# Attention on one Trainium2 core: sums of the softmax taken from the product with the values, copied and gathered off TensorE, with the transfers of one queue in another order

## The chip, the cores and the metric

The kernel runs on one core of a Trainium2 chip, as a single launch. The metric is device time in microseconds (us), and less is better. The engines named below are TensorE (PE; its weight loads are shown apart as PEld), VectorE (DVE), ScalarE (ACT), GpSimd (POOL) and SyncE (SP), whose queue here issues nearly all transfers of the stage that is changed.

## What is computed

The program is a small model of two layers: causal attention, a gated feed-forward net with 2:4 sparsity, a state space layer, and a mixture of experts, each behind a layer norm and added to its input. Only the first attention is touched: 8 sequences of 512 tokens, width 256, 16 heads of 16 columns.

```python
q = jnp.concatenate([q_sem, q_geo], axis=-1)
k = jnp.concatenate([k_sem, k_geo], axis=-1)
scores = jnp.einsum('bhqd,bhkd->bhqk', q, k).astype(jnp.float32) * scale
scores = jnp.where(causal, scores, jnp.finfo(jnp.float32).min)
attn = jax.nn.softmax(scores, axis=-1).astype(v.dtype)
out = jnp.einsum('bhqk,bhkd->bhqd', attn, v)
out = out.transpose(0, 2, 1, 3).reshape(B, S, ATTN_DIM)
return out @ Wo.T
```

## The kernel before

**Tiling.** `causal_attention` takes a batch (512 tokens) in two halves, f = 0 and 1, of 8 heads each. A half has four steps, t = 0 to 3, one for each pair of heads. Steps 0 and 1 belong to the first quad of four heads, steps 2 and 3 to the second. A step has three fills, j = 0 to 2, which share out the tiles of a 512 by 512 lower triangle. The middle six batches are a hardware loop over b with eight steps in it; the first and the last batch and two halves ahead of them are written out.

**What a step does.** PE writes the scores of this pair turned (keys on the partitions) into `p_st` (`turned_scores`, L384 in the trace), DVE limits the diagonal (`keep_past`, L580), and ACT takes the exponential into `pt_a`, `pt_b` or `pt_c` (`exponential`, L522). `p_st` is one buffer, so the turned scores of fill j + 1 wait for the exponential of fill j. Between them PE computes the scores of the pair two steps later the other way round (`scores`, L374 and L377, into `p_s`), and DVE takes their row maxima (`maximum`, L573).

**The path of the maxima.** A maximum has to stand in two extra rows of `qs` when its pair's turned scores begin. GpSimd splits it in two parts, DVE turns these (`turn_maxima`, L587, into `trn`), and SP moves them out to `max_dram` (`maxima_out`, L267) and back into rows of `qs` (`maxima_in`, L277). The first turned scores of a step wait for that.

**Queries and keys** of the next half go the same way: three transfers of a split projection to DRAM (`spread_rows`, L255), then two back (`stack`, L262) into `qs` or `ks`. All of them stand in SP's queue in the order of the code, and a wait in it holds up all that is behind. In step 0 SP issues the maxima out, the stack of the queries, the maxima in and the spread of the keys; in step 1 the maxima out, the stack of the keys, the maxima in.

**Values and sums.** `weigh` (L414) multiplies the exponentials of a quad by its values into `p_o`, and by `ones` into `p_sum`. It runs for fill 0 at the end of steps 1 and 3, and for fills 1 and 2 in the step behind. In step 0 of the next half DVE takes the reciprocal of `p_sum` in two parts (L625, L633) and multiplies `p_o` by it into `ot` (L636). The output product of a batch (`project_out`, L422) follows in steps 2 and 3 of the half f = 0 of the next batch, into the banks a and c, and `add_residual` (L600) adds the input. In step 3 it waits for ACT's copies of the turned values out of bank c (`v_pad`, L543).

In the profile the program's names have the prefix `a_`: `a_psst` is `p_st`, `a_pss` `p_s`, `a_pso` `p_o`, `a_pssum` `p_sum`, `a_psa` and `a_psb` the banks a and c.

## Time and profile before

| what | us |
| --- | --- |
| median of three runs | 6276.34 (6274.32 to 6280.89) |
| the profiled execution, whole | 6271.52 |
| its span | 6269.7 |
| first scores of the attention to its last output product | 95.78 to 803.06 |
| PE busy in the stretch 155 to 765 | 533.57 of 610.00 |
| DVE, ACT, POOL busy in it | 368.07, 178.62, 89.51 |

The attention is about a ninth of the span. The rest of the program has the same code in both kernels. In a view by time (the timeline) a row gives the start, the length, the engine and line, and in brackets how long the engine had been idle and which engine or transfer ended that. The rows of SPq are issues of transfers: their length is that of the issue, not of the transfer.

### The profile page before, as it was taken

How to read it: one execution, taken by the hardware profiler on the slowest of the kernel's cores; microseconds unless marked ns; L12 is line 12 of the kernel's file. 1: busy time of each engine (PE TensorE's matmuls, PEld its weight loads, DVE VectorE, ACT ScalarE, POOL GpSimd, SP SyncE). 2: the span in 40 equal slices, each digit the busy share in tenths (PEclk: the TensorE clock that was granted, in tenths of full speed). 3: DMA queues.
4: the chain of work that ended last, by engine and by line, in shares of the span. 5: the costliest groups of instructions: out<-in, count | busy, mean ns of one | idle time of the engine just before them, and what ended most of it. 6: DMA issues, size and time to landing. Idle time of an engine off the chain costs nothing. (4 is left out here: it accounts for less than half of the span.)

```text
span 6269.7 us, 129594 instructions
## 1 busy us (share of the span) xinstructions
PE 5619.0 (90%) x41820; PEld 4006.3 (64%) x41820; DVE 4504.9 (72%) x6855; ACT 3469.1 (55%) x4692; POOL 3610.0 (58%) x4085
## 2 busy tenths in 40 slices
PE   5888858747999999999999999999999999985599
PEld 3444447535777777777777777777777777763487
DVE  4666555545888888888888888888888888844444
ACT  2233222134777777777777777777777777731122
POOL 2111100005888888888888888888888888830000
PEclk8899779868999999999999999999999999987799
DMA  3333210122111111111111111111111111122100
GB/s 91 91 93 84 68 61 24 47 71 66 31 28 33 29 30 28 32 29 30 29 30 32 28 31 28 32 29 30 28 33 29 30 28 31 29 77 74 42 24 20
DMA packets 428605, 263.10 MB, mean 42 GB/s; under 512 B 264740, under 2 KB 359524, under 8 KB 427652
## 3 DMA queue, kind: packets, MB, share of 16 engines
q1 hardware_dynamic: 420100, 253.98, 15.7%
q10 hardware_dynamic: 8448, 8.39, 0.4%
q8 instruction: 32, 0.52, 0.0%
q14 instruction: 25, 0.20, 0.0%
HBM read 186.73 MB, written 66.85 MB: 40 GB/s over the span
## 5 line engine op out<-in xcount | busy, mean ns | idle before, releaser
L1537 ACT ACTIVATE ss_r<-ss_pssum,ss_eps 128x512 f32<-128x512 f32 x512 | 352.8, 689 | 900.5 <-PE ss_pssum L1468 900.5
L1597 DVE SCALAR_TENSOR_TENSOR ss_psb<-ss_psb,ss_norm,ss_r 128x512 f32<-128x512 f32 x512 | 362.8, 754 | 446.2 <-ACT ss_r L1539 446.2
L1468 PE MATMUL ss_pssum<-ss_sq,ss_pairssum 128*128 128x512 f32 x1024 | 570.9, 639 | 57.1 <-DVE ss_fr L1585 57.0
L1349 POOL TENSOR_TENSOR ss_sq<-ss_sq 128x512 f32<-128x512 f32 x256 | 329.7, 1288 | 452.5 <-ACT ss_sq L1546 452.5
L48 PE MATMUL ss_psb<-x_hi,ss_whi 128*128 x1024 | 529.5, 517 | 4.4 <-DVE ss_fr L1585 4.4
L1449 PE MATMUL ss_psse<-ss_rot 64*128 64x128 f32 x8224 | 529.4, 279 | 1.2 <-POOL ss_rot L1331 1.2
L1379 POOL TENSOR_TENSOR ss_own<-ident,ss_tk 128x512 f32<-128x512 f32 x512 | 524.8, 1047 | 0.0
L1449 PEld LDWEIGHTS ss_psse<-ss_rot 64*128 64x128 f32 x8224 | 480.1, 188 | 44.4 <-issue 42.9
L48 PE MATMUL ss_psc<-x_hi,ss_whi 128*128 x1024 | 504.9, 493 | 0.0
L50 PE MATMUL ss_psb<-x_hi,ss_wlo 128*128 x1024 | 404.1, 395 | 0.0
L49 PE MATMUL ss_psc<-x_lo,ss_whi 128*128 x1024 | 403.6, 394 | 0.0
L1339 POOL TENSOR_TENSOR ss_sq<-ss_sq 128x512 f32<-128x512 f32 x256 | 325.1, 1270 | 135.0 <-ACT ss_sq L1553 135.0
L50 PE MATMUL ss_psc<-x_hi,ss_wlo 128*128 x1024 | 402.2, 393 | 0.0
L49 PE MATMUL ss_psb<-x_lo,ss_whi 128*128 x1024 | 402.0, 393 | 0.0
L1304 POOL MEMSET ss_rot<- 128x4096 f32 x1 | 3.5, 3512 | 669.5 <-POOLq L2018 669.5
L1458 PE MATMUL ss_psm<-ss_xe,ss_bt 128*128 128x16 f32 x3084 | 388.9, 264 | 0.0
L1458 PEld LDWEIGHTS ss_psm<-ss_xe,ss_bt 128*128 128x128 f32 x3084 | 363.9, 191 | 31.2 <-issue 0.2
L1597 DVE SCALAR_TENSOR_TENSOR ss_psc<-ss_psc,ss_norm,ss_r 128x512 f32<-128x512 f32 x512 | 361.5, 752 | 0.0
L1619 DVE TENSOR_TENSOR ss_gm<-ss_psse,ss_dec 128x1024 f32<-128x1024 f32 x257 | 314.7, 1224 | 41.7 <-POOL ss_dec L1340 41.7
L1539 ACT ACTIVATE ss_r<-ss_r 128x512 f32<-128x512 f32 x512 | 324.1, 633 | 16.3
L1373 POOL TENSOR_TENSOR ss_rot<-ss_rot,ss_tmp 128x512 f32<-128x512 f32 x256 | 333.0, 1301 | 0.0
L1519 ACT ACT_TABLE_LOAD x257 | 329.7, 1283 | 4.5
(354 smaller groups left out, 15646.1 us busy)
## 6 DMA issues: line engine op xcount, KB each, us to landing
ss_dtb<-time_steps SPq DMA_DIRECT2D x516, 128.0 KB, 2.8
ss_wraw<-in_w_state SPq DMA_DIRECT2D x264, 80.0 KB, 2.3
head_rows<-a_yhi SPq DMA_DIRECT2D x64, 256.0 KB, 3.5
a_qs<-head_rows SPq DMA_DIRECT2D x32, 384.0 KB, 5.7
a_ks<-head_rows SPq DMA_DIRECT2D x32, 384.0 KB, 5.6
ss_xp<-x_heads SPq DMA_DIRECT2D x33, 256.0 KB, 4.2
y_heads<-ss_yo SPq DMA_DIRECT2D x132, 64.0 KB, 2.4
head_rows<-a_ylo SPq DMA_DIRECT2D x32, 256.0 KB, 3.7
```

What stands on the lines that cost most here:

```text
L48: nc.tensor.matmul(out, w_hi, x_hi, start=first, stop=False)
L49: nc.tensor.matmul(out, w_hi, x_lo, start=False, stop=False)
L50: return nc.tensor.matmul(out, w_lo, x_hi, start=False, stop=last)
L1349: G.tensor_tensor(sq[:, 0, 0], sq[:, 0, 0], sq[:, 0, 1], ALU.add).then_inc(ss_b, 1)
L1373: G.tensor_tensor(rot[:, j, 0], rot[:, j, 0], tmp[:, 0, 0], ALU.add)
L1379: last = G.tensor_tensor(own[:, h * TPB:(h + 1) * TPB], g.ident[:].rearrange("p (o t) -> p o t", o=1).broadcast_to([P, TPB, P]), at_diagon ...
L1449: last = M(p_se[:, h * TPB + c, :], rot[at, 1 - j, e, cols], rot[at, 1 - j, 2 + e, cols], start=e == 0, stop=e == 1)
L1458: last = M(p_m[:, (c * 2 + e) * PW:(c * 2 + e + 1) * PW], bt[:, 2 if e else j, c, :], xe[:, 1 - j, c, :], start=True, stop=True)
L1468: M(p_sum[:], pairs_sum[:], sq[:, q, 0], start=True, stop=True).then_inc((sum_b, sum_c)[q], 1)
L1519: A(trig[:, j, 0], fr[:], ACT.Sin, scale=UNDER_TURN)
L1537: A(r[:, q], p_sum[:], ACT.Ln, scale=1.0 / N1, bias=eps[:, 0:1]).then_inc(ln, 1)
L1597: link.mark(S(bank[:, e, :], bank[:, e, :], norm[:, 2 * q + e:2 * q + e + 1], r[:, q], ALU.mult, ALU.mult))
```

## The change

**Values and sums in one product.** `v_pad` is filled with 1.0, so the 16 columns beside a head's values give its sum. Each quad has a bank of its own (`p_o[0]`, `p_o[1]`), and the product with `ones` is gone. What is left has values and sums in alternate strips of 16 rows.

**Normalisation.** ACT copies a quad's bank to `o_sb`, and once more, times a column of zeros and ones, to `o_own` (`take`), in step 3 for the first quad and in step 0 of the next half for the second. SP moves the sums to their values' rows by four transfers a quad (`gather_sums`). GpSimd adds the two parts of `o_own` (step 1), DVE takes the reciprocals, one at the end of step 1 and one in step 2, and multiplies in step 2.

**Maxima.** DVE turns them right behind the first `keep_past` of a step, ahead of the first `maximum`. They come in by two transfers of two rows instead of four of one, and ahead of the stack of the queries. The stack of the keys moves from step 1 to step 0, behind the spread of the keys.

**Output.** `project_out` now runs in step 3 of f = 0 and step 0 of f = 1, both into bank c; the store moves from step 0 to step 1 of f = 1. One more step is written out at the end.

```diff
@@ -203,3 +203,6 @@
         vt, v_pad = sb("vt", [P, SEQ]), sb("vpad", [P, TPB, 2, 2, 4, 2 * DH])
-        ones, nil = sb("ones", [P, 2, 2 * DH]), sb("nil", [P, 2, TPB])
+        nil = sb("nil", [P, 2, TPB])
+        o_sb, sums = sb("osb", [P, 2, SEQ]), sb("sums", [P, SEQ])
+        o_own, o_all = sb("oown", [P, 2, SEQ]), sb("oall", [P, SEQ])
+        strips, own = sb("strips", [P, 2, 4]), sb("own", [P, 2])
         rec, ot = sb("rec", [P, SEQ]), sb("ot", [P, KD, SEQ])
@@ -208,3 +211,3 @@
         p_st, p_s = ps("st", [P, 2, SEQ]), ps("s", [P, 2, SEQ])
-        p_o, p_sum = ps("o", [P, SEQ]), ps("sum", [P, SEQ])
+        p_o = [ps(f"o{q}", [P, SEQ]) for q in range(2)]
         p_ab = [ps(n, [P, SEQ]) for n in "ab"]
@@ -235,2 +238,3 @@
                 step(BATCH, 0, t, BATCH)
+            step(BATCH, 1, 0, BATCH)
 
@@ -274,6 +278,11 @@
                 for e in range(2):
-                    for s in range(2):
-                        at = 64 * e + KS + s
-                        sp.dma_start(qs[at:at + 1, f, u, :].bitcast(FP32).rearrange("o (i a r) -> o i a r", i=TPB, a=TPB),
-                                     columns[8 * e + 4 * s:8 * e + 4 * s + 4].unsqueeze(0)).then_inc(max_in[p], 16)
+                    at = 64 * e + KS
+                    sp.dma_start(qs[at:at + 2, f, u, :].bitcast(FP32).rearrange("s (i a r) -> s i a r", i=TPB, a=TPB),
+                                 columns[8 * e:8 * e + 8].rearrange("(s i) a r -> s i a r", s=2)).then_inc(max_in[p], 16)
+
+            def gather_sums(half, quad):
+                sp.wait_ge(o_copied, half * 2 + quad + 1)
+                for c in range(4):
+                    to, at = 32 * c + DH * quad, 32 * c + DH * (1 - quad)
+                    sp.dma_start(sums[to:to + DH, :], o_sb[at:at + DH, quad, :]).then_inc(sums_in, 16)
 
@@ -284,4 +293,2 @@
                     maxima_out(b, 4 * f + t + 1)
-                if t < 2 and is_half(half + 1):
-                    stack(*after, t)
                 if is_pair(4 * half + t + 1):
@@ -289,6 +296,12 @@
                 if t == 0 and is_half(half + 1):
+                    stack(*after, 0)
                     spread_rows(*after, 1)
+                    stack(*after, 1)
                 if t == 2 and is_half(half + 2):
                     spread_rows(b + 1, f, 0)
-                if f == 1 and t == 0 and 1 <= n < BATCH:
+                if t == 3 and is_half(half):
+                    gather_sums(b * 2 + f, 0)
+                if t == 0 and is_half(half - 1):
+                    gather_sums(b * 2 + f - 1, 1)
+                if f == 1 and t == 1 and 1 <= n < BATCH:
                     before = b - 1
...
@@ -313,3 +326,3 @@
             G.memset(top2[:].bitcast(FP32), 0.0)
-            G.memset(v_pad[:], 0.0).then_inc(cleared, 1)
+            G.memset(v_pad[:], 1.0).then_inc(cleared, 1)
             G.memset(qs[:].bitcast(FP32), 0.0).then_inc(cleared, 1)
@@ -335,2 +348,6 @@
                     rest(*after, 1)
+                if t == 1 and is_half(half - 1):
+                    pool.wait_ge(o_masked, (b * 2 + f) * 2)
+                    at_least(pool, ot_done, b * 2 + f - 1)
+                    G.tensor_tensor(o_all[:], o_own[:, 0], o_own[:, 1], ALU.add).then_inc(merged, 1)
                 if t == 1 and is_half(half + 2):
...
@@ -411,6 +428,5 @@
                     width = SEQ - kt * P
-                    for psum, left in ((p_o, lambda c: v_pad[:, kt, f, quad, c, :]), (p_sum, lambda c: ones[:, quad, :])):
-                        for c in range(4):
-                            last = M(psum[32 * c:32 * c + 32, kt * P:SEQ], left(c), pt[:, c // 2, c % 2, at:at + width],
-                                     start=quad == 0 and j == 0, stop=quad == 1 and j == 2, skip_group_check=True)
+                    for c in range(4):
+                        last = M(p_o[quad][32 * c:32 * c + 32, kt * P:SEQ], v_pad[:, kt, f, quad, c, :], pt[:, c // 2, c % 2, at:at + width],
+                                 start=j == 0, stop=j == 2, skip_group_check=True)
                 last.then_inc(pv_done, 1)
...
@@ -444,3 +460,3 @@
                     project(b + 1, f * HALF, a).then_inc(proj_done, 1)
-                if t == 3 and outs:
+                if f == 0 and t == 3 and outs:
                     if is_half(half + 1):
@@ -448,6 +464,4 @@
                     pe.wait_ge(ot_done, b * 2)
-                    project_out(b, 1, c)
+                    project_out(b, 0, c)
                 if t == 3 and is_half(half + 2):
-                    if outs:
-                        pe.wait_ge(res_done, b * 2 - 1)
                     pe.wait_ge(rope_read, counts(2) + 1)
@@ -462,16 +476,15 @@
                     weigh(ef, eq, 2)
+                if f == 1 and t == 0 and outs:
+                    if is_half(half + 1):
+                        pe.wait_ge(rope_read, counts(1) + 4)
+                    pe.wait_ge(res_done, b * 2 - 1)
+                    project_out(b, 1, c)
                 if t == 1 and is_half(half + 2):
                     at_least(pe, rope_read, counts(1) + 4)
+                    if f == 1 and outs:
+                        pe.wait_ge(res_done, b * 2)
                     project(b + 1, f * HALF + P, c).then_inc(proj_done, 1)
-                if t == 2 and outs:
-                    if is_half(half + 2):
-                        pe.wait_ge(rope_read, counts(2) + 1)
-                    if is_half(half + 1):
-                        pe.wait_ge(vt_ready, b * 2 + f + 2)
-                    at_least(pe, res_done, b * 2 - 2)
-                    pe.wait_ge(ot_done, b * 2)
-                    project_out(b, 0, a)
                 if t == 3 and is_half(half + 2):
-                    if outs:
-                        pe.wait_ge(res_done, b * 2)
+                    if f == 0 and outs:
+                        pe.wait_ge(res_done, b * 2 - 1)
                     at_least(pe, vpad_done, b * 2 + f + 2)
@@ -488,3 +501,3 @@
                         pe.wait_ge(vpad_done, b * 2 + f + 1)
-                        at_least(pe, ot_done, b * 2 + f)
+                    at_least(pe, o_masked, b * 4 + f * 2 - 1 + t // 2)
                     weigh(f, t // 2, 0)
...
@@ -523,2 +537,9 @@
 
+            def take(half, quad):
+                act.wait_ge(pv_done, (half * 2 + quad + 1) * FILLS)
+                at_least(act, rec_done, half)
+                at_least(act, merged, half)
+                A(o_sb[:, quad], p_o[quad][:], ACT.Copy).then_inc(o_copied, 1)
+                A(o_own[:, quad], p_o[quad][:], ACT.Copy, scale=own[:, quad:quad + 1]).then_inc(o_masked, 1)
+
             def high(b, f, kind):
@@ -534,2 +555,4 @@
                     exponential(b, f, t, 0)
+                if t == 3 and here:
+                    take(b * 2 + f, 0)
                 if t == 0 and is_half(half + 1):
@@ -548,2 +571,4 @@
                     exponential(b, f, t, 2)
+                if t == 0 and is_half(half - 1):
+                    take(b * 2 + f - 1, 1)
                 if t == 0 and is_half(half + 1):
@@ -561,6 +586,8 @@
             V.tensor_scalar(limit[:], above_f[:, 1, :], 1.5e38, 2.0, ALU.add, ALU.mult).then_inc(t_loaded, 1)
-            V.memset(ones[:], 0.0).then_inc(t_loaded, 1)
-            dve.wait_ge(t_loaded, 51)
-            V.memset(ones[:, 0, 0:DH], 1.0)
-            V.memset(ones[:, 1, DH:2 * DH], 1.0).then_inc(t_loaded, 1)
+            for q in range(2):
+                V.tensor_reduce(strips[:, q], g.ident[:].rearrange("p (c w) -> p c w", w=2 * DH)[:, :, DH * q:DH * (q + 1)], AX.X, ALU.add).then_inc(t_loaded, 1)
+            dve.wait_ge(t_loaded, 52)
+            for q in range(2):
+                last = V.tensor_reduce(own[:, q:q + 1], strips[:, q], AX.X, ALU.add)
+            last.then_inc(t_loaded, 1)
 
...
@@ -604,3 +631,3 @@
                 ahead = is_pair(4 * half + t + 2)
-                outs = f == 0 and 1 <= n <= BATCH
+                outs = 1 <= n <= BATCH
                 here = is_half(half)
@@ -608,8 +635,8 @@
                     keep_past(b, f, t, 0)
-                if ahead:
-                    maximum(b, f, t, 0)
                 if is_pair(4 * half + t + 1):
                     turn_maxima(b, 4 * f + t + 1)
-                if t == 3 and outs:
-                    add_residual(b, 1)
+                if ahead:
+                    maximum(b, f, t, 0)
+                if f == 0 and t == 3 and outs:
+                    add_residual(b, 0)
                 if here:
@@ -622,16 +649,19 @@
                     turn(b + 1, f, t // 2, 1)
-                if t == 0 and is_half(half - 1):
-                    dve.wait_ge(pv_done, (b * 2 + f) * 2 * FILLS)
-                    V.reciprocal(rec[:, 0:SEQ // 2], p_sum[:, 0:SEQ // 2])
+                if f == 1 and t == 0 and outs:
+                    add_residual(b, 1)
+                if t == 2 and is_half(half - 1):
+                    V.reciprocal(rec[:, SEQ // 2:SEQ], sums[:, SEQ // 2:SEQ]).then_inc(rec_done, 1)
                 if here:
                     keep_past(b, f, t, 2)
-                if t == 2 and outs:
-                    add_residual(b, 0)
                 if ahead:
                     maximum(b, f, t, 2)
-                if t == 0 and is_half(half - 1):
-                    V.reciprocal(rec[:, SEQ // 2:SEQ], p_sum[:, SEQ // 2:SEQ]).then_inc(rec_done, 1)
+                if t == 1 and is_half(half - 1):
+                    dve.wait_ge(sums_in, (b * 2 + f) * 128)
+                    at_least(dve, ot_done, b * 2 + f - 1)
+                    V.reciprocal(rec[:, 0:SEQ // 2], sums[:, 0:SEQ // 2])
+                if t == 2 and is_half(half - 1):
                     at_least(dve, wo_done, b * 2 if f else b * 2 - 2)
+                    dve.wait_ge(merged, b * 2 + f)
                     dve.wait_ge(rec_done, b * 2 + f)
-                    V.tensor_tensor(ot[:, 1 - f, :], p_o[:], rec[:], ALU.mult).then_inc(ot_done, 1)
+                    V.tensor_tensor(ot[:, 1 - f, :], o_all[:], rec[:], ALU.mult).then_inc(ot_done, 1)
 
```

SP's queue in the hardware loop, from the end of the maxima in of step 0 to those of step 1 in the first half. `maxima` and `head_rows` are scratch tensors in DRAM; a wait for `ln0_stats` is one for the split projection (a number used again). Before:

```order
L277 DMA a_qs<-maxima 1x16x32 x3
L252 REGISTER_ALU
L255 DMA head_rows<-a_yhi 128x512 [waits ln0_stats]
L255 DMA head_rows<-a_yhi 128x512
L255 DMA head_rows<-a_ylo 128x512
L266 REGISTER_ALU
L267 DMA maxima<-a_trn 128x32 [waits a0_turned]
L262 DMA a_ks<-head_rows 48x4x512 [waits a0_kspread]
L262 DMA a_ks<-head_rows 48x4x512
L272 ISA
L277 DMA a_qs<-maxima 1x16x32 [waits a0_maxout0]
L277 DMA a_qs<-maxima 1x16x32 x3
```

After, from the spread of the keys on; the maxima in of step 0 and the stack of the queries stand right ahead of it:

```order
L259 DMA head_rows<-a_yhi 128x512 [waits ln0_stats]
L259 DMA head_rows<-a_yhi 128x512
L259 DMA head_rows<-a_ylo 128x512
L266 DMA a_ks<-head_rows 48x4x512 [waits a0_kspread]
L266 DMA a_ks<-head_rows 48x4x512
L284 ISA
L287 DMA a_sums<-a_osb 16x512 [waits a0_ocopied]
L287 DMA a_sums<-a_osb 16x512 x3
L270 REGISTER_ALU
L271 DMA maxima<-a_trn 128x32 [waits a0_turned]
L276 ISA
L280 DMA a_qs<-maxima 2x16x32 [waits a0_maxout0]
```

The stack of the keys, with its wait for the spread, and the gathering of the sums moved ahead of the maxima out of step 1.

DVE in the same loop, the change from step 0 to step 1, before (waits for `a0_st` are for turned scores, those for `ln0_hi` for scores):

```order
L633 RECIPROCAL a_rec<-a_pssum 128x256
L218 REGISTER_ALU
L636 TENSOR_TENSOR a_ot<-a_pso,a_rec 128x512 [waits a0_rec,a0_wo]
L577 ISA
L580 TENSOR_TENSOR a_psst<-a_psst,a_limit 128x2x128 [waits a0_st]
L569 ISA
L573 TENSOR_REDUCE a_top<-a_pss 128x2 [waits a0_mlo,ln0_hi]
L573 TENSOR_REDUCE a_top<-a_pss 128x2
L218 ISA [waits a0_mlo]
L587 STREAM_TRANSPOSE a_trn<-a_top 128x32 [waits a0_maxout0]
```

After, the change from step 1 to step 2:

```order
L607 TENSOR_TENSOR a_psst<-a_psst,a_limit 128x2x128 [waits a0_st]
L596 REGISTER_ALU
L600 TENSOR_REDUCE a_top<-a_pss 128x2 [waits ln0_hi]
L659 ISA
L221 REGISTER_ALU [waits a0_sumsin]
L661 RECIPROCAL a_rec<-a_sums 128x256 [waits a0_ot]
L607 TENSOR_TENSOR a_psst<-a_psst,a_limit 128x2x128 [waits a0_st]
L612 REGISTER_ALU
L614 STREAM_TRANSPOSE a_trn<-a_top 128x32 [waits a0_maxout1,a0_mlo]
L596 ISA
L600 TENSOR_REDUCE a_top<-a_pss 128x2 [waits a0_mlo,ln0_hi]
L600 TENSOR_REDUCE a_top<-a_pss 128x2
```

The transpose moved from behind the step's two first reductions to ahead of them, and a reciprocal with a wait for the gathered sums now stands at the end of step 1.

## Rows read from the trace of the kernel before

**Rows 1.** Windows: span, busy time of PE, PEld, DVE, ACT, POOL; clock, DMA.

```profile
155.00:765.00 610.00, 533.57 (x3756) 279.72 (x3748) 368.07 (x623) 178.62 (x238) 89.51 (x167) 0.88 0.36 86
...
460.40:474.70 14.30, 14.29 (x52) 6.79 (x52) 6.05 (x11) 2.65 (x3) 1.68 (x3) 0.53 0.33 62
```

**Rows 2.** Waits of PE from 155 to 765: total us, times, longest.

```profile
PE a_psst L384 <- DMA a_qs<-maxima: 55.4, 28, 3.4
PE a_psb L422 <- ACT a_vpad L543: 7.4, 7, 1.1
```

**Rows 3.** Timeline of PE: first turned scores of a step, each row one step.

```profile
217.18 0.50 PE L384 MATMUL a_psst<-a_qs,a_ks 50*128 50x512 f32 x2 [0.59 <-DMA a_qs<-maxima]
...
388.45 0.50 PE L384 MATMUL a_psst<-a_qs,a_ks 50*128 50x512 f32 x2
...
397.53 0.49 PE L384 MATMUL a_psst<-a_qs,a_ks 50*128 50x512 f32 x2 [0.21 <-ACT a_ptc L522]
...
410.38 0.49 PE L384 MATMUL a_psst<-a_qs,a_ks 50*128 50x512 f32 x2
...
421.61 0.49 PE L384 MATMUL a_psst<-a_qs,a_ks 50*128 50x512 f32 x2 [2.87 <-DMA a_qs<-maxima]
...
432.51 0.50 PE L384 MATMUL a_psst<-a_qs,a_ks 50*128 50x512 f32 x2 [0.97 <-DMA a_qs<-maxima]
...
440.80 0.50 PE L384 MATMUL a_psst<-a_qs,a_ks 50*128 50x512 f32 x2 [0.92 <-DMA a_qs<-maxima]
...
449.36 0.50 PE L384 MATMUL a_psst<-a_qs,a_ks 50*128 50x512 f32 x2
...
460.41 0.50 PE L384 MATMUL a_psst<-a_qs,a_ks 50*128 50x512 f32 x2 [2.68 <-DMA a_qs<-maxima]
...
474.74 0.53 PE L384 MATMUL a_psst<-a_qs,a_ks 50*128 50x512 f32 x2
...
728.79 0.49 PE L384 MATMUL a_psst<-a_qs,a_ks 50*128 50x512 f32 x2 [1.55 <-DMA a_qs<-maxima]
```

**Rows 4.** Timeline of PE: products with ones, and a third fill's turned scores.

```profile
416.23 0.39 PE L384 MATMUL a_psst<-a_qs,a_ks 50*128 50x256 f32 x2 [0.35 <-ACT a_ptb L522]
...
430.50 1.04 PE L414 MATMUL a_pssum<-a_pta,a_ones 128*32 128x512 f32 x8
...
472.87 1.93 PE L414 MATMUL a_pssum<-a_pta,a_ones 128*32 128x512 f32 x8
```

**Rows 5.** Timeline of SP's queue: issues of transfers in three steps and ahead.

```profile
80.39 0.81 SPq L262 DMA_DIRECT2D a_qs<-head_rows  x2
...
88.70 0.81 SPq L262 DMA_DIRECT2D a_ks<-head_rows  x2
...
413.42 0.32 SPq L267 DMA_DIRECT2D maxima<-a_trn  x1
413.87 0.83 SPq L262 DMA_DIRECT2D a_qs<-head_rows  x2
...
425.01 0.91 SPq L262 DMA_DIRECT2D a_ks<-head_rows  x2
426.06 2.57 SPq L277 DMA_DIRECT2D a_qs<-maxima  x4
435.56 0.35 SPq L267 DMA_DIRECT2D maxima<-a_trn  x1
437.01 2.57 SPq L277 DMA_DIRECT2D a_qs<-maxima  x4
```

**Rows 6.** Timeline of PE: start of the first scores of the stage.

```profile
95.48 0.37 PE L374 MATMUL a_pss<-a_above,ident 128*128 128x128 bf16 x2 [12.96 <-DMA a_ks<-head_rows]
```

**Rows 7.** Timelines of DVE and ACT: a limit, a reciprocal and a copy.

```profile
410.92 0.43 DVE L580 TENSOR_TENSOR a_psst<-a_psst,a_limit 128x256 f32<-128x256 f32 x1 [1.45 <-PE a_psst L384]
...
416.08 1.75 DVE L625 RECIPROCAL a_rec<-a_pssum 128x256 f32<-128x256 f32 x1
418.77 0.60 ACT L552 ACTIVATE a_vt<-a_psa 128x512 f32<-128x512 f32 x1
```

More of the change, by code:

```diff
@@ L178, in causal_attention @@
     s_done, max_done, mhi_done, mlo_done = sem("s"), sem("max"), sem("mhi"), sem("mlo")
-    keep_done = sem("keep")
+    keep_done, o_copied, sums_in, o_masked, merged = (sem(n) for n in ("keep", "ocopied", "sumsin", "omasked", "merged"))
     st_done, exp_done, pv_done, rec_done, ot_done = sem("st"), sem("exp"), sem("pv"), sem("rec"), sem("ot")
@@ L305, in _ @@
             for p in range(2):
-                sp.wait_ge(max_in[p], PAIRS0 // 2 * 64)
+                sp.wait_ge(max_in[p], PAIRS0 // 2 * 32)
         @block.gpsimd
@@ L400, in turned_scores @@
                 if j == 0:
-                    pe.wait_ge(max_in[t % 2], b * 256 + ((4 * f + t) // 2 + 1) * 64)
+                    pe.wait_ge(max_in[t % 2], b * 128 + ((4 * f + t) // 2 + 1) * 32)
                 at_least(pe, exp_done, (b * 8 + 4 * f + t) * FILLS + j)
@@ L501, in _ @@
             pe.wait_ge(w_split, 4)
-            pe.wait_ge(t_loaded, 16 * 3 + 4)
+            pe.wait_ge(t_loaded, 16 * 3 + 5)
             pe.wait_ge(cleared, 3)
@@ L515, in _ @@
             act.wait_ge(cleared, 3)
+            act.wait_ge(t_loaded, 16 * 3 + 5)
             def exponential(b, f, t, j):
@@ L599, in add_residual @@
                 rows = out[:, part * 2:part * 2 + 2, :]
-                V.tensor_tensor(rows, p_ab[part][:].rearrange("p (n d) -> p n d", n=2), rows, ALU.add).then_inc(res_done, 1)
+                V.tensor_tensor(rows, p_ab[1][:].rearrange("p (n d) -> p n d", n=2), rows, ALU.add).then_inc(res_done, 1)
             def step(b, f, t, n):
@@ L604, in step @@
                 ahead = is_pair(4 * half + t + 2)
-                outs = f == 0 and 1 <= n <= BATCH
+                outs = 1 <= n <= BATCH
                 here = is_half(half)
@@ L608, in step @@
                     keep_past(b, f, t, 0)
+                if is_pair(4 * half + t + 1):
+                    turn_maxima(b, 4 * f + t + 1)
                 if ahead:
                     maximum(b, f, t, 0)
-                if is_pair(4 * half + t + 1):
-                    turn_maxima(b, 4 * f + t + 1)
-                if t == 3 and outs:
-                    add_residual(b, 1)
+                if f == 0 and t == 3 and outs:
+                    add_residual(b, 0)
                 if here:
```

## The prediction

> **What bounds the kernel now.** The view by windows comes first: over most of the attention PE is busy 533.57 of 610.00 us, at a mean clock of 0.88, DVE 368.07, the others less [rows 1]. So PE is the first bound, and what it waits for is the second: 28 waits for the maxima's rows of `qs`, 55.4 us in all, and 7 for the copies of `v_pad`, 7.4 us [rows 2]. The timeline puts them in place [rows 3]. A batch takes 85.3 us (six periods from 217.18 to 728.79); I work in the one from 388.45 to 474.74, 86.29 us. Steps 2 and 3 of f = 0 take 9.08 and 12.85. Then steps 0 and 1 of f = 1 take 22.13 together, with waits of 2.87 and 0.97 for the maxima at their ends; steps 2 and 3 take 8.29 (0.92 of it such a wait) and 8.56; steps 0 and 1 of the next batch take 25.38.
>
> Why are the maxima late at the end of step 0? In SP's queue their way in stands behind the stack of the queries [rows 5]: out at 413.42, the stack at 413.87, and the step waits until 421.61. In step 1 it is behind the stack of the keys (425.01): the maxima are issued from 426.06 to 428.63, and step 2 starts at 432.51, 3.9 us later. With no stack ahead (437.01) it was 440.80, 1.2 us after the last issue ended. So transfers of one queue land about in order.
>
> A wait is followed by a low clock. Step 1 from 460.41, behind a wait of 2.68, ran at a mean clock of 0.53, mostly the lower of the levels 1.2 and 2.4 GHz [rows 1], and took 14.33 where the one from 421.61 took 10.90, of which 0.97 was a wait.
>
> **Products with ones (gain).** A product with ones of 512 columns costs PE some 0.9 us (1.04 with its tail) at full clock and 1.9 at the lower [rows 4]. A quad has three such lots: fill 0, fill 1 (384 + 128 columns) and fill 2 (256 columns, half the price). For fill 0 and fill 1 PE is the last to be ready, so 0.9 each comes off; for fill 2 the next turned scores wait 0.35 for an exponential already [rows 4], and nothing comes off.
>
> **Steps 2 and 3.** The maxima are turned earlier and come in by two issues, which takes away the wait of 0.92: 8.29 - 0.92 - 0.87 = 6.5. Against that a reciprocal of 1.75 [rows 7] now stands ahead of the third `keep_past`, where DVE has about 0.5 free: +1.25. Step 2 becomes 7.8. In f = 0 it is the same, since the output product left that step: 9.08 to 7.8. Step 3 of f = 1: 8.56 - 0.9 + 0.1 (the exponential is next in line) = 7.75. In step 3 of f = 0 the output product waits for `v_pad` [rows 2], and ACT now makes two copies of 0.6 [rows 7] ahead of it: 12.85 - 0.9 + 1.2 = 13.15.
>
> **Steps 0 and 1.** Were PE the bound, step 0 of f = 1 would take 11.23 - 2.87 - 0.9 + 1.1 (the output product moved here, less the lot and the wait that it covers) = 8.6, step 1 10.90 - 0.97 - 0.95 = 9.0, together 17.6; 16.4 in f = 0. But SP's queue has to be walked through. Count from the start of step 0. The limit starts 0.54 later and takes 0.43 [rows 3, 7]; with the transpose, the maxima go out at 1.2 (3.04 before). In 1.45 later [rows 5], at 2.65; two issues of 0.64 end at 3.95. Step 1 has its maxima in time: that wait goes. Stack of the queries at 4.0. Then come the spread of the keys and the stack of the keys, which waits for the spread. At the head of the stage the same sequence stands bare: queries at 80.39, keys at 88.70, 8.3 us later [rows 5]. So the stack of the keys is issued at 12.3. It landed 6.8 later there (95.48) [rows 6], here at 19.1. Behind it are four issues of `gather_sums`, at the stack's 0.46 each, and only then, at 15.0, the maxima out, which land behind the stack: about 19.5. In from 19.5; with two issues, landing 1.9 behind the start of the last: 22.1. **Step 2 starts 22.2 us after step 0**, in both halves, whatever PE saved. What comes off PE in these two steps, and the first wait, come back as one wait of 4.6 to 5.8 us at the end of step 1. DVE's reciprocal there waits for the sums (landed by about 20) and is done by 22, under the same wait; on GpSimd the merge is ahead of `total`, in time by 10 us. Bounds: with 1.28 for an issue of two rows, twice that of one, 24.1; if the maxima were not held behind the stack, 15.0 + 1.45 + 0.64 + 1.9 = 19.0. I take 0.64, by the nearest row.
>
> The Trainium skill, page "DMA: Bandwidth & Descriptors", section "Why a DMA increments its semaphore by 16 and not by 1", says that a transfer runs on the largest number of engines up to 16 that divides the slowest dimension of both sides. By it two rows would use 2 engines where one row of 4 by 4 pieces used 4, which speaks against joining the rows: I estimate 0.5 us later on each way in, 6283 in all; no trace here shows it.
>
> **The clock (loss).** The new wait is longer than those of 2.7 to 2.9 that the low clock followed, and what follows it is step 2. The lower level makes PE's work some 1.44 times as long (14.33 to 9.93). In step 2 it is the bound for the first third and has slack behind: +2.0 if the whole step is slow, 0 if none, +4.5 if step 3 is slow too. I take 2.0, since step 1 was slow throughout after one such wait and in part after another.
>
> **Sum.** One batch: 7.8 + 13.15 + 22.2 + 7.8 + 7.75 + 22.2 = 80.9, against 86.29, and the period is 1.0 longer than the mean: 4.4 less. The clock gives back 4.0. So 0.4 less a batch, 3 us in 7.5 batches. At the end, `take`, gathering and two output products in one bank cost some 2 us more. That makes 6271.5 - 1 = 6270.5 for the profiled execution; the median is 4.8 above it: **6275 us, no change**.
>
> **Rivals.**
> 1. The likeliest: the wait moves to the end of step 1, with a clock cost of 1.2 to 2.8 a half. 6263 to 6287. Chance 0.40.
> 2. Slower, by the clock: behind the long wait steps 2 and 3 both run at the lower level, 4.5 a half instead of 2.0: 2.5 x 15 = 37 us more, 6312. For it: the 14.33 of the step from 460.41. Against: the step from 421.61 recovered. It decides from about 8 us of low clock after the wait. Chance 0.15.
> 3. Slower, by the issue: two rows cost 1.28 in an issue: 24.1 instead of 22.2, 1.9 x 15 = 28 us, 6303. For it: an issue has the same number of small pieces a row. Chance 0.16.
> 4. Faster, by the clock: it stays up, or falls within the wait and is back: 0.4 a half, 1.6 x 15 = 24 us less, 6251. Chance 0.15.
> 5. Faster, by the transfers: the maxima aren't held up by the stack of the keys. Steps 0 and 1 take 19.0, 48 us less, and a gap of 2 us costs the clock half: 6275 - 48 - 15 = 6212. Against it: the 3.9 us of 428.63 to 432.51. Chance 0.14.
>
> **How the numbers follow.** A measurement of this kernel can tell 0.2%, 12.6 us, from no change. Faster by more than that: cases 4 and 5 and a little of 1, 0.30. Slower: 2 and 3 and a little of 1, 0.33. Within: 0.37. The range 6235 to 6316 leaves out case 5 and the far part of 2; case 1 alone has 6263 to 6287.
>
> **What would show it.** Right: no wait for maxima at the start of step 1, one of 4 to 6 us at the start of step 2; 22 us from step 0 to step 2; the stack of the keys issued some 12 us into step 0; the maxima out of step 1 issued only after the gathering. Steps 2 near 8 and 10 by the clock. Wrong: step 2 starting 18 to 20 us after step 0 (case 5), issues of the maxima well over 0.64 (case 3), a clock of 1.0 in step 2 (case 4), a wait of DVE for the gathered sums that turned scores then wait for, or a `v_pad` wait much over 2.3.

## The result, and the profile after

The changed kernel took 6326.14 us (median of four runs, 6324.81 to 6330.77) against 6275.33 for the kernel before in the same job: a ratio of 1.0083, with a 95% interval of 1.0068 to 1.0098. It is slower by 51 us, where no change was forecast, and 10 us beyond the end of the range. Its profiled execution has a span of 6323.0.

The first view is again that by windows: span, busy time of PE, PEld, DVE, ACT and POOL, then the clock, the share of the transfer engines and GB/s. The first row is most of the attention, the second steps 0 and 1 of one half, the third steps 2 and 3 behind them.

```profile
155.00:800.00 645.00, 512.37 (x2822) 267.51 (x2823) 362.59 (x615) 208.27 (x294) 112.22 (x180) 0.74 0.37 86
431.40:454.40 23.00, 16.19 (x106) 9.00 (x106) 12.95 (x22) 7.36 (x10) 5.14 (x10) 0.91 0.57 114
454.40:474.90 20.50, 19.77 (x98) 9.78 (x98) 12.83 (x22) 7.42 (x11) 3.03 (x4) 0.60 0.30 94
```

PE has less work, 79% of the time against 87%, and the mean clock of the stage fell from 0.88 [rows 1] to 0.74. Steps 2 and 3 ran at 0.60. The waits of PE from 155 to 800 (total, times, longest):

```profile
PE a_psst L401 <- DMA a_qs<-maxima: 102.8, 14, 9.2
PE a_psb L438 <- ACT a_vpad L566: 10.6, 7, 1.5
```

And one of DVE, in the same view:

```profile
DVE a_rec L661 <- DMA a_sums<-a_osb: 64.9, 14, 6.5
```

This second one lies under the first: DVE's reciprocal of the gathered sums, in its timeline, is over at 497.09, and step 2 starts at 498.30, when the maxima have landed.

```profile
495.34 1.75 DVE L661 RECIPROCAL a_rec<-a_sums 128x256 f32<-128x256 f32 x1 [3.97 <-DMA a_sums<-a_osb]
```

The 28 waits for the maxima, 55.4 us in a window 35 us shorter [rows 2], have become 14, one for each half in the window, with nearly twice the time. The timeline of PE gives their place: the first turned scores of the steps of one batch, to be laid beside [rows 3].

```profile
406.16 0.79 PE L401 MATMUL a_psst<-a_qs,a_ks 50*128 50x512 f32 x2 [6.33 <-DMA a_qs<-maxima]
...
416.38 0.80 PE L401 MATMUL a_psst<-a_qs,a_ks 50*128 50x512 f32 x2 [0.69 <-ACT a_ptc L536]
...
431.34 0.51 PE L401 MATMUL a_psst<-a_qs,a_ks 50*128 50x512 f32 x2
...
439.87 0.50 PE L401 MATMUL a_psst<-a_qs,a_ks 50*128 50x512 f32 x2
...
454.44 0.80 PE L401 MATMUL a_psst<-a_qs,a_ks 50*128 50x512 f32 x2 [6.82 <-DMA a_qs<-maxima]
...
464.66 0.80 PE L401 MATMUL a_psst<-a_qs,a_ks 50*128 50x512 f32 x2 [0.69 <-ACT a_ptc L536]
...
474.87 0.50 PE L401 MATMUL a_psst<-a_qs,a_ks 50*128 50x512 f32 x2
...
483.24 0.79 PE L401 MATMUL a_psst<-a_qs,a_ks 50*128 50x512 f32 x2
...
498.30 0.80 PE L401 MATMUL a_psst<-a_qs,a_ks 50*128 50x512 f32 x2 [6.79 <-DMA a_qs<-maxima]
```

Step 1 (439.87, 483.24) begins without a wait. Step 2 (406.16, 454.44, 498.30) begins 23.1 to 23.4 us after step 0, behind a wait of 6.3 to 6.8 (6.3 to 9.2 over all 14), at the lower clock: 0.79 to 0.80 for an instruction that takes 0.50 at the upper one. SP's queue from the same step 0 (474.87) on shows what the maxima waited for:

```profile
476.00 0.32 SPq L271 DMA_DIRECT2D maxima<-a_trn  x1
477.41 1.35 SPq L280 DMA_DIRECT2D a_qs<-maxima  x2
478.90 0.82 SPq L266 DMA_DIRECT2D a_qs<-head_rows  x2
479.84 0.84 SPq L259 DMA_DIRECT2D head_rows<-a_yhi  x2
480.72 0.48 SPq L259 DMA_DIRECT2D head_rows<-a_ylo  x1
487.50 0.81 SPq L266 DMA_DIRECT2D a_ks<-head_rows  x2
488.45 2.45 SPq L287 DMA_DIRECT2D a_sums<-a_osb  x4
491.01 0.51 SPq L271 DMA_DIRECT2D maxima<-a_trn  x1
495.45 1.33 SPq L280 DMA_DIRECT2D a_qs<-maxima  x2
```

The queue stands from 481.2 to 487.50 for the spread of the keys. The maxima out, turned by 484.62, go at 491.01, behind the stack of the keys and the gathering, and take 4.4 us to land instead of the 1.45 of [rows 5].

| one batch, us | forecast | measured |
| --- | --- | --- |
| steps 0 and 1, f = 1 and f = 0 | 22.2 and 22.2 | 23.2 and 23.5 |
| steps 2, both | 15.6 and the clock | 20.4 |
| step 3, f = 1 and f = 0 | 7.75 and 13.15, and the clock | 10.1 and 14.6 |
| of this, beyond the 36.5 that steps 2 and 3 have without the clock by the forecast | 4.0 | 8.6 |
| sum | 84.9 | 91.7 |

The measured numbers are means over the six or seven halves of a kind between 198 and 772; the sum before was 85.3.

### The profile page after: what moved, and what is told of

The parts are those of the page before. It is cut to its first block and busy times, and to the rows that moved or that the text cites. A ratio compares the mean times of both kernels' runs of the same rounds, so it can differ in the third digit from the quotient of the medians.

```text
span 6323.0 us, 127791 instructions
## 1 busy us (share of the span) xinstructions
PE 5605.9 (89%) x40796; PEld 3999.4 (63%) x40796; DVE 4505.2 (71%) x6856; ACT 3501.7 (55%) x4756; POOL 3631.5 (57%) x4101
## 3 DMA queue, kind: packets, MB, share of 16 engines
q1 hardware_dynamic: 423428, 258.18, 16.3%
## 5 line engine op out<-in xcount | busy, mean ns | idle before, releaser
L1569 ACT ACTIVATE ss_r<-ss_r 128x512 f32<-128x512 f32 x512 | 324.0, 633 | 16.4
```

## The experiments

**Which theories.** The first: step 2 waits since the maxima stand behind the stack of the keys in SP's queue. The second: what makes steps 2 and 3 longer than forecast is the clock, and PE's idle time and lighter work set it. Rivals: the added copies, gathered sums and reciprocals hold the steps; PE's total work decides the time. Unused products, where an experiment has them, are further matrix products that PE writes into a free bank and nobody reads. The experiments ran in three groups, each beside the kernel before, whose medians there were 6277.08, 6276.81 and 6281.66 us; so a difference of a few us between runs of different groups says nothing.

**Order in the queue alone, in the kernel before.**

```diff
-                if t < 2 and is_half(half + 1):
-                    stack(*after, t)
...
                 if t == 0 and is_half(half + 1):
+                    stack(*after, 0)
                     spread_rows(*after, 1)
+                    stack(*after, 1)
```

> The kernel before with the changed order in SP's queue alone: maxima in ahead of the stack of the queries, the stack of the keys in step 0 behind the spread of the keys; products with ones, reciprocals, turn of the maxima and the four issues a maximum as before. Theory 1: step 2 starts about 26 us after step 0 (maxima out at 3.0, in to 7.0, keys at 15.4, landed 22.2, maxima in 22.7, landed 26.5) instead of 22 to 24, and steps 2 and 3 run at the lower clock: a batch some 11 to 15 us longer, the whole 6355 to 6390 us. Rival (the order in the queue costs nothing, the rest of the change is what costs): within 10 us of the kernel before.

It took 6358.9 us, a ratio to the kernel before of 1.0137 (1.0110 to 1.0163). PE's first turned scores of steps 0 and 2, in its timeline:

```profile
401.97 0.49 PE L384 MATMUL a_psst<-a_qs,a_ks 50*128 50x512 f32 x2
...
428.67 0.79 PE L384 MATMUL a_psst<-a_qs,a_ks 50*128 50x512 f32 x2 [8.90 <-DMA a_qs<-maxima]
...
451.37 0.50 PE L384 MATMUL a_psst<-a_qs,a_ks 50*128 50x512 f32 x2
...
478.87 0.80 PE L384 MATMUL a_psst<-a_qs,a_ks 50*128 50x512 f32 x2 [9.69 <-DMA a_qs<-maxima]
```

26.7 and 27.5 us from step 0 to step 2, with 26 expected. The total is in the expected range, but steps 2 and 3 do not both run at the lower clock. PE's waits for the maxima from 155 to 765, then three windows: 200 to 700, step 2 and step 3.

```profile
PE a_psst L384 <- DMA a_qs<-maxima: 113.6, 14, 11.2
```
```profile
200.00:700.00 500.00, 383.64 (x2768) 198.23 (x2757) 265.44 (x454) 131.38 (x176) 69.19 (x126) 0.87 0.32 77
428.67:439.97 11.30, 11.09 (x84) 5.72 (x85) 5.01 (x10) 3.17 (x4) 1.27 (x1) 0.77 0.20 72
439.97:451.37 11.40, 10.29 (x62) 5.91 (x62) 6.88 (x13) 3.20 (x5) 2.05 (x5) 1.00 0.01 2
```

The waits are longer than in the changed kernel, and yet the mean clock is 0.87. In 11 of 13 halves the clock is back 4.7 to 6.4 us into step 2 and stays up in step 3; in the changed kernel it stays low for 15 to 20 us from the start of step 2. This kernel still has the products with ones. None of the new copies or sums is in this kernel. The order of one queue alone costs 82 us; the rest of the change, with that order given, wins 33 of them back.

**The stack of the keys back in step 1, in the changed kernel.**

```diff
                     spread_rows(*after, 1)
+                if t == 1 and is_half(half + 1):
                     stack(*after, 1)
```

> The changed kernel with one move in SP's queue: the stack of the keys goes back to step 1, behind that step's maxima in; all else stays. Theory 1 (the maxima of step 1 are held behind the stack of the keys and the gathering): the wait of 6 to 9 us ahead of step 2 goes, at most 1 to 2 us are left there (keys themselves, landing 6.8 us after their issue), the clock stays near 0.95 in steps 2 and 3, a batch takes 72 to 76 us instead of 91.5, the whole about 6190 to 6210 us. Rival (the copies, the gathered sums or the reciprocals hold the steps): a wait of DVE for the sums or one of PE for ACT takes the place, a batch stays above 82 us, the whole above 6260 us.

6302.92 us, 1.0041 (1.0028 to 1.0053): 23 us better than the changed kernel, 100 short of what was expected. PE's waits:

```profile
PE a_pss L392 <- DMA a_ks<-head_rows: 66.1, 14, 5.4
PE a_psst L402 <- ACT a_ptc L537: 9.5, 14, 0.7
PE a_psst L402 <- DMA a_qs<-maxima: 9.5, 7, 2.5
```

The maxima are in time, or late by 0.8 to 2.5 us in half of the halves, as theory 1 has it. But now the keys are not: they are issued 6 us into step 1 (437.06, step 1 at 431.00), and the scores of step 2 wait until 443.64. That was named as 1 to 2 us and measured as 2.6 to 5.4. And the clock did not come back: 0.75 from 200 to 700. The rival's totals (a batch above 82 us, the whole above 6260) came true, but not its cause, that new work holds the steps: DVE's wait for the gathered sums is down to 0.7 us in all.

**The maxima first in both steps, in the kernel before.**

```diff
                 if is_pair(4 * half + t + 1):
                     maxima_out(b, 4 * f + t + 1)
-                if t < 2 and is_half(half + 1):
-                    stack(*after, t)
                 if is_pair(4 * half + t + 1):
                     maxima_in(b, 4 * f + t + 1)
+                if t < 2 and is_half(half + 1):
+                    stack(*after, t)
```

> The kernel before with the maxima in ahead of the stack in both steps, 0 and 1; the stack of the keys stays in step 1; nothing else. The waits for the maxima of 2.9 and 1.0 us go; the keys are issued 4 us after the maxima out of step 1 instead of 0.4 and land about 11 us later, where step 2's scores want them after 10.9: a wait of 1 to 3 us for the keys at step 2 takes the place. Steps 0 and 1 together 20 to 22 us instead of 22 to 25.4, the clock about as before since PE's work is the same: 6235 to 6265 us. Rival (the clock falls with the wait for the keys): the same as before or slower.

6344.87 us, 1.0107 (1.0090 to 1.0124), a miss by 80 us. SP's queue, step 1 having begun at 402.31:

```profile
406.26 0.32 SPq L267 DMA_DIRECT2D maxima<-a_trn  x1
410.44 2.57 SPq L277 DMA_DIRECT2D a_qs<-maxima  x4
413.05 0.93 SPq L262 DMA_DIRECT2D a_ks<-head_rows  x2
```

With the wait of step 0 gone, the maxima out of step 1 (406.26) meet the stack of the queries and the spread of the keys, which are still moving: 4.2 us to land, where I counted 1.4. The keys are issued 10.7 us into step 1 instead of the 4 expected, and PE waits for them and for the maxima:

```profile
PE a_pss L374 <- DMA a_ks<-head_rows: 68.6, 13, 5.7
PE a_psst L384 <- DMA a_qs<-maxima: 37.7, 15, 4.3
```

106 us against 55.4 [rows 2]. So the stack ahead of the maxima was no oversight of the kernel before: three bulk transfers and two small ones have to pass one after another, and this order, with the small ones first, pushes the bulk back by a round trip to DRAM.

**The clock: unused products ahead of step 2, in the changed kernel.** In this edit and in the others with unused products, the product is the same, with another number and, ahead of step 1, bank `c` and a wait for `counts(1) + 4`.

```diff
+                if t == 2 and here and is_half(half + 2):
+                    pe.wait_ge(rope_read, counts(2) + 1)
+                    for _ in range(28):
+                        M(a[:], w_hi[:, 0, 0:P], g.x_hi[:, 0, 0:SEQ], start=True, stop=True)
                 if here:
                     turned_scores(b, f, t, 0)
```

> The changed kernel with 28 products of 512 columns more, about 6 us at full clock, which PE computes into a free bank ahead of step 2 in 14 of 16 halves, while it would wait for the maxima; nothing uses them. SP's order stays. Theory of the clock (steps 2 and 3 lose some 4 us a half to the lower clock behind the wait): from step 0 to step 2 still 23 us, but steps 2 of 7.8 to 8.5 instead of 10.2 us, steps 3 of 7.8 instead of 10.1 in f = 1 and about 13 in f = 0, clock near 1.0 there, the whole some 45 to 60 us shorter than the changed kernel: 6265 to 6280 us. Rival (steps 2 and 3 are long because of the added work on ACT and DVE, not of the clock): steps stay at 10, the whole the same as the changed kernel or slower.

6284.32 us, 1.0009 (0.9999 to 1.0019): 42 us less than the changed kernel, with more work on PE and the same queue. In PE's timeline, the unused products, then steps 2 and 3:

```profile
424.76 6.64 PE L454 MATMUL a_psa<-x_hi,a_whi 128*128 128x512 f32 x28
431.93 0.49 PE L401 MATMUL a_psst<-a_qs,a_ks 50*128 50x512 f32 x2 [0.53 <-DMA a_qs<-maxima]
...
439.70 0.80 PE L401 MATMUL a_psst<-a_qs,a_ks 50*128 50x512 f32 x2 [1.27 <-ACT a_ptc L540]
```

The window from 200 to 700, by the columns of the first view:

```profile
200.00:700.00 500.00, 455.11 (x2668) 267.36 (x2666) 300.31 (x510) 169.38 (x240) 95.86 (x150) 0.91 0.41 95
```

Step 2 takes 7.7 to 7.8 us in 11 of 14 halves (8.7 and 8.8 in two), just what the forecast had without the clock, where the changed kernel takes 10.2. Step 3 falls short of what was expected: 9.2 to 11.9 us in f = 1 and 13.5 to 14.2 in f = 0, instead of 7.8 and 13. In each of these the clock falls again, though no wait for the maxima is longer than 2.1 us. Only in the first half of all does it stay up through step 3, which takes 7.8 us. The two windows are that step 3 and a later one, both without an output product:

```profile
143.01:150.81 7.80, 7.70 (x45) 4.16 (x46) 5.87 (x12) 4.26 (x7) 1.44 (x3) 1.00 0.14 35
439.70:451.58 11.88, 11.88 (x46) 6.43 (x46) 6.33 (x12) 4.26 (x7) 1.70 (x3) 0.57 0.17 51
```

So the clock is worth at least 42 us here, most of it in steps 2.

**The products with ones alone, out of the kernel before.** This run leaves the sums of the softmax out; the reciprocals read the bank of the values.

```diff
-                    for psum, left in ((p_o, lambda c: v_pad[:, kt, f, quad, c, :]), (p_sum, lambda c: ones[:, quad, :])):
+                    for psum, left in ((p_o, lambda c: v_pad[:, kt, f, quad, c, :]),):
...
-                    V.reciprocal(rec[:, 0:SEQ // 2], p_sum[:, 0:SEQ // 2])
+                    V.reciprocal(rec[:, 0:SEQ // 2], p_o[:, 0:SEQ // 2])
```

> The kernel before without the products with ones (the sums are left out: the reciprocals read the bank of the values instead), the order of the queue unchanged. Theory 1 (PE's relief is lost where the maxima are awaited): PE's work falls by 70 us, but steps 0 and 1 stay at 22 to 24 us; only the steps without such a wait shrink, by 0.9 each: 15 to 35 us less, 6240 to 6260 us. Rival (PE is the bound throughout): 50 to 70 us less, 6205 to 6225 us.

6296.22 us, 1.0030 (1.0020 to 1.0040): slower, by 19 us, where both theories had a gain. The same window for the kernel before and for this one:

```profile
200.00:700.00 500.00, 439.64 (x3088) 233.51 (x3086) 302.70 (x514) 148.48 (x199) 77.02 (x140) 0.89 0.38 89
```
```profile
200.00:700.00 500.00, 423.43 (x2270) 226.55 (x2263) 291.84 (x492) 141.46 (x190) 74.20 (x133) 0.78 0.35 83
```

The clock fell from 0.89 to 0.78. The waits for the maxima grew from 55.4 to 75.8 us, since PE came to them sooner, and the work between ran slower by more than was taken out of it. Longer waits alone don't do this: with the order of the queue alone changed they were 113.6 us, and with the maxima first 37.7 and 68.6 for the keys, at a clock of 0.87 both times.

**The same with unused products at the waits**, 16 ahead of step 1 and 8 ahead of step 2; the sums are left out here too.

> The kernel before without the products with ones (sums left out, as in the run before this), with unused products instead, 16 ahead of step 1 and 8 ahead of step 2, where PE would wait. If taking the products with ones away made the kernel slower (6296 against 6277 us) because the clock fell to 0.78, giving PE work at the waits alone brings the clock back above 0.9 and the time below that of the kernel before: 6245 to 6265 us. If something else made it slower (the banks, the order of the products), the time stays near 6296 us.

6276.57 us, 1.0001 (0.9992 to 1.0011), clock 0.90. The 19 us came back with the clock, which bears out that it was the cause; the further 10 to 30 us expected did not come. The unused products take 5.9 us a half (mostly 3.79 and 2.11), some 83 us in 14 halves, so PE has at least as much to do as before; the run shows what work on PE is worth to the clock, and not what a lighter PE at the full clock would give.

**Unused products in the kernel before**, 12 ahead of step 1 and 4 ahead of step 2.

> The kernel before with products of 512 columns that nothing uses, 12 of them (2.6 us at full clock) ahead of step 1 and 4 (0.9 us) ahead of step 2 in 14 of 16 halves, where PE waits for the maxima. Theory of the clock (the lower clock after the wait at the end of step 0 costs time in the kernel before too, some 99 us of its records lie there): the clock rises from 0.88 to near 1.0 in the stage, steps 0 and 1 of f = 0 fall from 24.3 to 22 us, the whole 15 to 35 us less than the kernel before: 6242 to 6262 us. Rival (more work on PE is more time, the clock falls anyway): the same or up to 10 us more.

6270.29 us, 0.9989 (0.9979 to 0.9999), clock 0.96: some 7 us, about a quarter of the mean expected, and hardly clear of the noise. From 200 to 700 steps 0 and 1 have no lower clock left (41 us of it are in steps 2 and 3), and together they still take 21.8 to 23.1 us: the queue holds them, as far as the unused products in them don't. So in the kernel before the clock costs little, as its slow stretches lie mostly in steps which the queue holds anyway.

**The keys on ACT's queue, in the changed kernel.**

```diff
+            def stack_keys(b, f):
+                act.wait_ge(spread[1], b * 96 + f * 48 + 48)
+                rows = stack_dram[1, f].rearrange("(u e r) q -> e r u q", e=2, r=KS)
+                for e in range(2):
+                    act.dma_start(ks[64 * e:64 * e + KS, f, :, :].bitcast(FP32), rows[e]).then_inc(k_in[f], 16)
...
                     exponential(b, f, t, 1)
+                if t == 1 and is_half(half + 1):
+                    stack_keys(*after)
+                if here:
                     exponential(b, f, t, 2)
```

> The changed kernel with the stack of the keys issued from ACT's queue in step 1, behind ACT's second exponential, instead of SP's; so neither the maxima nor the keys stand behind one another. Theory of the queue: maxima in time for step 2 (a wait under 1 us), the keys land about 20.5 us after step 0 began and the scores of step 2 wait 2 to 4 us for them; steps 0 and 1 take 18 to 20 us with that. Theory of the clock with it: it stays at 0.75 to 0.8, since PE still has less work, steps 2 and 3 stay near 10, the whole 6265 to 6295 us. Rival (the clock recovers once the waits are short): 6200 to 6230 us.

6277.37 us, 1.0002 (0.9992 to 1.0011): 49 us less than the changed kernel, the same as the kernel before, with the clock at 0.76. The total was as expected, the wait was not: 3.5 to 5.2 us for the maxima, and for the keys (3.0) in one half only. The timelines of ACT's queue, SP's queue and PE:

```profile
423.93 0.81 ACTq L548 DMA_DIRECT2D a_ks<-head_rows  x2
...
424.17 1.35 SPq L280 DMA_DIRECT2D a_qs<-maxima  x2
...
430.90 0.80 PE L400 MATMUL a_psst<-a_qs,a_ks 50*128 50x512 f32 x2 [3.71 <-DMA a_qs<-maxima]
```

Issued beside the keys from another engine's queue, the maxima land 6.7 us after their issue begins, against 3.8 with nothing beside them [rows 3, 5], where they even were four transfers and not two. A second queue spares the wait in the first; it doesn't get small transfers past a large one. The Trainium skill, page "DMA: Bandwidth & Descriptors", section "Issuing engines are not separate DMA queues", says as much: transfers of all engines end up on the same transfer engines and interleave. The trace agrees.

**Four transfers of one row, on top of that.** `maxima_in` as in the kernel before.

> The kernel with the keys' stack on ACT's queue, and the maxima in by four transfers of one row again instead of two of two. There the maxima are issued at about the same time as the keys and land 6.7 us later. Theory of the joined rows (two rows of 32 small pieces go over fewer of the transfer engines than one row of 16 does, so each piece waits for more of the keys' packets): the wait of 3.7 us ahead of step 2 falls to 0 to 2 us in spite of 1.3 us more issue. Rival (the number of engines doesn't matter): the wait grows by 1 to 1.3 us. The time moves by 2 us at most a half either way, the clock may hide it: 6255 to 6290 us.

6306.1 us, 1.0041 (1.0027 to 1.0055). The wait at step 2 grew to 4.6 to 5.2 in f = 1 (6.6 once), by about the rival's 1 to 1.3, and to 6.1 to 8.1 in f = 0, by more; what adds to it there is not shown. The first step of what I put forward, that two rows over fewer transfer engines cost more than four, falls: joining them was right. The rule that the prediction cited for it is not seen to matter here.

**Unused products with the keys on ACT's queue.** Behind the first turned scores of step 2, 12 of them:

> The kernel of the run above (keys on ACT's queue) with 12 unused products of 512 columns (2.6 us at full clock) in step 2, between its first turned scores and its first scores, where it waits for the keys. Theory of the clock: steps 2 and 3 fall from 10 to about 8 us, the clock rises above 0.9, the whole 6200 to 6240 us, faster than both kernels. Rival (PE's total work decides the time): the same as the run above or up to 25 us more.

6307.29 us, 1.0047 (1.0030 to 1.0064), 30 us more than without them. In PE's timeline they stand behind the wait, at the lower clock:

```profile
443.94 0.80 PE L400 MATMUL a_psst<-a_qs,a_ks 50*128 50x512 f32 x2 [3.68 <-DMA a_qs<-maxima]
444.66 5.31 PE L455 MATMUL a_psa<-x_hi,a_whi 128*128 128x512 f32 x12
```

They take 5.3 us, and step 2 becomes 3.0 longer, 13.2 us instead of 10.2; step 3 is no shorter, and the clock from 200 to 700 is 0.82, not above 0.9. Ahead of the first turned scores, 16 of them:

> The kernel with the keys' stack on ACT's queue, and 16 unused products of 512 columns (3.4 us at full clock) ahead of the first turned scores of step 2, where PE waits 3.7 us for the maxima, instead of behind them. Theory of the clock (what precedes step 2 decides its clock, not PE's total work): step 2 takes 7.8 us instead of 10.2, step 3 falls too, the wait stays covered, the whole 30 to 50 us less than the run with the keys on ACT's queue: 6228 to 6248 us, faster than both kernels. Rival (unused work costs as much as the clock gives): the same as that run, 6270 to 6285 us.

**6241.70 us, 0.9935 (0.9919 to 0.9952), faster than both kernels.** Products, step 2 and step 3 in PE's timeline:

```profile
484.47 3.92 PE L453 MATMUL a_psa<-x_hi,a_whi 128*128 128x512 f32 x16
488.32 0.50 PE L400 MATMUL a_psst<-a_qs,a_ks 50*128 50x512 f32 x2
...
496.10 0.50 PE L400 MATMUL a_psst<-a_qs,a_ks 50*128 50x512 f32 x2 [1.27 <-ACT a_ptc L539]
```

And its window from 200 to 700:

```profile
200.00:700.00 500.00, 450.88 (x2669) 254.36 (x2667) 317.44 (x539) 180.83 (x256) 99.89 (x158) 0.88 0.42 99
```

The expected 7.8 us came in step 2, but step 3 did not fall with it: 9.2 to 11.9 us in f = 1, where the run without the unused products has 9.8 to 10.1, and 13.6 to 14.8 in f = 0. The same kind of work, on the other side of the wait, makes 66 us of difference (16 products ahead of it, 12 behind it). With four transfers of one row and 10 products:

> Both at once: keys on ACT's queue, maxima in by four transfers, and 10 unused products (2.2 us) ahead of step 2. If the joined rows cost time and the clock is kept: 5 to 20 us below the run with 16 unused products and two transfers, 6215 to 6235 us. If the joined rows cost nothing: 5 to 20 us above it.

6306.43 us, 1.0044 (1.0030 to 1.0059), against an expected 6215 to 6235: joined rows are worth more than expected, and 10 products do not fill a wait of 4.7 to 7 us.

## Why the prediction was wrong

**What bounds the kernel: right.** The waits for the maxima, their place, and the queue as their cause hold; the run with the queue's order alone settles it. Their length was put at 4.6 to 5.8 us and measured as 6.3 to 9.2, since PE's own part of steps 0 and 1 took some 16.3 and 15.2 us instead of 17.6 and 16.4, and the queue 1.0 to 1.3 us more than forecast.

**The queue (steps 0 and 1): right in kind, 1.0 to 1.3 us short.** The forecast for the sequence from step 0 on was: out at 1.2, in at 2.65, queries at 4.0, keys at 12.3, maxima out at 15.0, in at 19.5, step 2 at 22.2. The trace has 1.13, 2.54, 4.03, 12.63, 16.14, 20.58 and 23.43. Each issue of `gather_sums` took 0.61 us where the stack's 0.46 was taken as the nearest row. That makes 0.6 of the 1.2 us. An issue of two rows took 0.67, so rival 3 falls.

**Steps 2 and 3 without the clock: right where it can be seen.** 7.8 us is what the kernel with filled waits shows. It also has one step 3 without an output product at the full clock, of 7.8 us, where the forecast had 7.75; for the 13.15 of f = 0 no run shows one.

**The clock: this step failed.** It was sized at 2.0 a half, with 4.5 as the far end for steps 2 and 3 both slow. Measured it is 4.3 a half: 91.7 - 46.7 (steps 0 and 1) = 45.0 for steps 2 and 3 of both halves, against 36.5 without the clock, so 8.6 a batch. Of these, 4.8 are in steps 2 and 2.3 in step 3 of f = 1, where the kernel with filled waits shows 7.8 us at the full clock for each; the 1.4 in step 3 of f = 0 are put down to the clock because it is low for 7 to 10 us of it, and that is not shown by itself. It is rival 2, which had a chance of 0.15, and with the queue's 2.3 a batch on top it left the range. Adding the terms up: 6.8 a batch over the forecast, 51 us in 7.5 batches.

The slip was to take the wait for the cause and to read its price off the kernel before, where the clock was low for at most 13.6 us behind a wait of 2.7. The wait's length is not what decides: in the run with the queue's order alone, behind waits of 8.7 to 11.2, the clock was back 4.7 to 6.4 us into step 2 in 11 of 13 halves (11.1 and 18.1 in the other two). In the changed kernel, where the products with ones are gone, it stayed low through all of step 2 and half to two thirds of step 3, in every half. The factor of 1.44 was low as well: the step from 421.61, taken as the fast one, had itself 3.4 us at the lower level.

**What I left out.** Taking the products with ones away was counted as pure gain. The run without them shows a loss of 19 us in the kernel before, with the clock down from 0.89 to 0.78, while the two runs that kept them and waited for 106 and 114 us had 0.87. So what brought the clock down is the lighter work beside the waits, and not longer waits. PE's busy share doesn't tell the two apart: it was 85% of the window at 0.78 in the one, and 77% at 0.87 with the order alone.

**The end.** From the start of the last pair's step to the last addition of the residual the kernel before took 23.0 us (780.74 to 803.79), the changed one 27.8: 4.7 instead of 2 us more, most of it in DVE's wait of 8.4 us for the gathered sums.

**Not shown.** What it is in the lighter work that lets the clock fall, and why it still falls in step 3 of the fastest version, stays open. Sending the maxima from GpSimd's queue was not tried.

## What to carry to other kernels

When PE's work is cut in a stage in which PE also waits, count the wait's end first: if a transfer sets it, the cut buys nothing and the wait gets longer. Then ask what the clock does in the lighter stage, and price the whole stretch behind the wait at the lower level, not a part of it: here longer waits with the work kept cost the clock little, and less work cost it much. In a queue that also carries round trips of small transfers, moving a bulk transfer forward is safe only if nothing small is turned before it lands; and useless products can be worth more than they cost when PE computes them while it would wait; behind the wait they were a loss here.

## What was not expected of the hardware

- Less work on PE made a kernel slower: without the products with ones, expected as 70 us of work, it took 19 us more, with the granted clock from 0.89 to 0.78. Twice the waiting with these products kept left the clock at 0.87.
- 28 unused products in each of 14 halves made the changed kernel 42 us faster; 16, with the keys on another queue, gave 36 us over the same kernel without them, though PE then computed more.
- Small transfers issued from SP beside a 768 KB stack issued from ACT landed 6.7 us after their issue began (two transfers), against 3.8 alone (four).
- An issue of a transfer within SBUF of 16 rows of 2 KB took 0.61 us, more than that of 192 rows of 2 KB from DRAM at 0.41.
